# Layer 2 scan: the four blocks of squares of a unit added on GpSimd, one block summed by TensorE instead of four

## What is computed

```python
def mamba2(x, in_w, conv_w, conv_b, dt_bias, A_log, D, gnorm_w, out_w):
    zxbcdt = x @ in_w.T
    z, xBC, dt = ...                       # 512, 512 + 2 * 128 and 8 columns
    dt = softplus(dt + dt_bias)
    xBC = silu(conv(xBC) + conv_b)         # 4 taps along the tokens
    y = ssd(xh, dt, A, B, C) + xh * D[None, None, :, None]
    y = y.reshape(b, l, D_INNER)           # D_INNER = 512
    y = rmsnorm(y * silu(z), gnorm_w)
    return y @ out_w.T

def rmsnorm(x, w):
    return x * rsqrt(mean(x * x, axis=-1) + EPS) * w
```

## Time and profile before

| | |
|---|---|
| time, median of 3 runs | 3643.48 us (3633.23 to 3653.20) |
| span of the profiled execution | 3570.1 us |
| mean granted TensorE clock | 0.932 |
| TensorE, matmul | 3198.0 us busy, 90% |
| TensorE, weight loads | 1856.8 us, 52% |
| VectorE | 2185.0 us, 61% |
| ScalarE | 1801.6 us, 50% |
| GpSimd | 1033.9 us, 29% |
| the scan of layer 2 | about 1735 to 2066 us of the span |

### The profile page before, as it was taken

The page is one execution under the profiler, slowest core; times in us unless marked ns, Lnnn a source line. Parts: engine busy times, 40 slices in busy tenths (PEclk is TensorE's granted clock), DMA queues, the critical chain, the costliest instruction groups (busy, mean ns, idle before and its releaser), DMA issues. The chain is left out here.

```text
span 3570.1 us, 54815 instructions
## 1 busy us (share of the span) xinstructions
PE 3198.0 (90%) x18704; PEld 1856.8 (52%) x18724; DVE 2185.0 (61%) x4458; ACT 1801.6 (50%) x4178; POOL 1033.9 (29%) x1198
## 2 busy tenths in 40 slices
PE   6978849999989899968999988787999999998989
PEld 3655638878756566634456666353233333332656
DVE  4765575455666566675655365335888888884750
ACT  4957723333233344444655444113677777776531
POOL 2535464433350122232444521114111111111300
PEclk8988869999988899998999999898899999999999
DMA  9200056666440000032000041233000000001100
GB/s 333 79 9 1 1 204 199 206 196 187 140 117 1 24 1 1 1 126 85 1 1 1 1 171 48 107 102 106 10 19 19 17 11 19 19 10 50 48 4 21
DMA packets 161108, 240.54 MB, mean 67 GB/s; under 512 B 22771, under 2 KB 136052, under 8 KB 156948
## 3 DMA queue, kind: packets, MB, share of 16 engines
q1 hardware_dynamic: 147012, 199.27, 17.0%
q0 software_dynamic: 13824, 37.77, 3.3%
HBM read 131.97 MB, written 104.99 MB: 66 GB/s over the span
## 5 line engine op out<-in xcount | busy, mean ns | idle before, releaser
L4437 DVE TENSOR_REDUCE peaks<-ps 128x1 f32<-128x1024 f32 x512 | 608.6, 1220 | 152.0 <-PE ps L4379 146.8
L4465 ACT ACTIVATE attn<-ps 128x512 f32<-128x512 f32 x1024 | 535.5, 602 | 118.3 <-PE ps L4370 116.5
L4379 PE MATMUL ps<-keys,queries 96*128 96x512 bf16 x1024 | 391.0, 387 | 5.1 <-DVE peaks L4437 4.9
L4370 PE MATMUL ps<-queries,keys 99*128 99x512 bf16 x1024 | 390.3, 384 | 3.5 <-ACT attn L4465 2.7
L4392 PE MATMUL ps<-attn,head_values 128*32 128x512 f32 x2048 | 272.3, 604 | 0.0
L4370 PEld LDWEIGHTS ps<-queries,keys 99*128 99x128 bf16 x1024 | 99.1, 98 | 306.7 <-ACT attn L4465 222.3
L1187 POOL TENSOR_TENSOR attn_w<-attn_w,attn_share 128x512 f32<-128x512 f32 x128 | 131.7, 1050 | 378.7 <-DVE attn_share L1033 378.7
L2039 PE MATMUL ps<-experts,tileT 128*128 x884 | 228.2, 380 | 0.0
L2240 DVE COPY normed<-ps 128x256 f32<-128x256 f32 x221 | 93.7, 424 | 181.6 <-PE ps L2055 179.7
L4520 POOL CAST peak_parts<-peak 128x4 bf16<-128x4 f32 x64 | 12.3, 193 | 516.6 <-DVE peak L4443 516.6
L2039 PEld LDWEIGHTS ps<-experts,tileT 128*128 128x128 f32 x884 | 151.0, 191 | 15.4 <-issue 0.4
(11 more groups left out here) (697 smaller groups left out, 7106.6 us busy)
## 6 DMA issues: line engine op xcount, KB each, us to landing
tile_in<-routed_rows SPq DMA_DIRECT2D x244, 128.0 KB, 2.3
expert_rows<-normed SPq DMA_DIRECT2D x221, 128.0 KB, 2.2
routed_rows<-zeros SPq DMA_DIRECT2D x2, 8064.0 KB, 45.3
experts<-in_L_ffn_experts SPq DMA_DIRECT2D x4, 3072.0 KB, 20.8
routed_rows<-zeros SPq DMA_DIRECT2D x1, 12160.0 KB, 61.1
kT<-L_xattn_keys SPq DMA_DIRECT2D x8, 1024.0 KB, 7.0
v<-L_xattn_values SPq DMA_DIRECT2D x8, 1024.0 KB, 7.7
experts<-in_L_ffn_experts SPq DMA_DIRECT2D x8, 1024.0 KB
```

The lines of the kernel that those rows point to most:

```text
L4370: nc.tensor.matmul(bank(("score", n)), keys[h % 3][0:DEEP, sl(kt)], queries[h % 3][0:DEEP, sl(c, CHUNK)], start=True, stop=True).then_inc( ...
L4379: last = nc.tensor.matmul(k.ps[:, SB + p % PB, :], queries[h % 3][0:ROWS, sl(t)], keys[h % 3][0:ROWS, sl(c, CHUNK)], start=True, stop=True)
L4437: v.tensor_reduce(peaks[:, r % 2, i // 2, i % 2:i % 2 + 1], k.ps[:, at:at + 2, :], AX.XY, ALU.max).then_inc(s["maxed"], 1)
L4465: nc.scalar.activation(attn[:, n % RING, :], bank(("score", n)), ACT.Exp, scale=1.0 / 16.0).then_inc(s["read"], 1)
```

## The change

`squares` has two blocks instead of four. GpSimd squares block 0 into the first and each further block into the second, which it then adds to the first, so that a unit has seven instructions where it had four (`SQUARINGS = 2 * M - 1`), each with a count on `squared`. Before it squares block 2 or 3 into the second block it waits until the add before has read it; before an add it waits for its square. TensorE waits for all seven and does four products, one for each tile, with the summed block.

```diff
--- before.py
+++ after.py
@@ -3658,7 +3658,8 @@
         inputs = sb(k, stack, "inputs", [P, GROUP, INNER])
         lasting = sb(k, stack, "lasting", [P, HEADS, GROUP, P])
         y = [sb(k, stack, "y", [P, M, GT]) for _ in range(2)]
-        squares = sb(k, stack, "squares", [P, M, GT])
+        squares = sb(k, stack, "squares", [P, 2, GT])
+        SQUARINGS = 2 * M - 1
         scale = [sb(k, stack, "scale", [P, GROUP]) for _ in range(2)]
 
         def is_unit(u):
@@ -3790,12 +3791,11 @@
                     last.then_inc(s["mixed"], 1)
 
                 def square_sums(u):
-                    need(pe, "squared", M * (u + 1))
+                    need(pe, "squared", SQUARINGS * (u + 1))
                     need(pe, "meant", u - 1)
                     for j in range(GROUP):
-                        for m in range(M):
-                            last = nc.tensor.matmul(k.ps[:, 7, 128 + GROUP * (u % 2) + j:129 + GROUP * (u % 2) + j], squares[:, m, sl(j)],
-                                                    k.ones[:, 0:1], start=m == 0, stop=m == M - 1)
+                        last = nc.tensor.matmul(k.ps[:, 7, 128 + GROUP * (u % 2) + j:129 + GROUP * (u % 2) + j], squares[:, 0, sl(j)],
+                                                k.ones[:, 0:1], start=True, stop=True)
                     last.then_inc(s["square_sums"], 1)
 
                 def leave(u, j):
@@ -3938,7 +3938,12 @@
                             if m == 0:
                                 need(pool, "square_sums", u)
                             pool.wait_ge(s["multiplied"], M * u + m + 1)
-                            g_.tensor_tensor(squares[:, m, :], y[u % 2][:, m, :], y[u % 2][:, m, :], ALU.mult).then_inc(s["squared"], 1)
+                            if m >= 2:
+                                pool.wait_ge(s["squared"], SQUARINGS * u + 2 * m - 1)
+                            g_.tensor_tensor(squares[:, min(m, 1), :], y[u % 2][:, m, :], y[u % 2][:, m, :], ALU.mult).then_inc(s["squared"], 1)
+                            if m >= 1:
+                                pool.wait_ge(s["squared"], SQUARINGS * u + 2 * m)
+                                g_.tensor_tensor(squares[:, 0, :], squares[:, 0, :], squares[:, 1, :], ALU.add).then_inc(s["squared"], 1)
 
             @block.vector
             def _(dve):
```

## The result

The changed kernel took 3602.25 us in the median of four runs (3595.79 to 3605.78), the kernel before 3643.69 us beside it; ratio 0.9887, interval 0.9866 to 0.9908. Repeated against the kernel before, it came out at 0.9903 (0.9882 to 0.9924) and 0.9916 (0.9897 to 0.9936). So it is faster by 30 to 41 us. The trace puts 35.2 us of this into the scan.

What follows compares the result with a forecast made beforehand. It took TensorE to bound the layer 2 scan, busy 296.4 of 306 us. Records 14.6, unit 7 and tail 5.0 and clock 11.7 sum to 31.3 us off 3643.5: 3612 us, range 3601 to 3634.

Steps and rivals of the forecast that it cites:

- Removed records: TensorE's sums in the first six units: 8 of 32 records remain, 17.0 us off, 2.4 us back waiting for exponentials.
- The adds: GpSimd, layer 2 scan: 24 adds of 1.27 us, 4.05 us per unit with waits, hidden except behind the last unit.
- Unit 7 and the tail: Last unit and what follows: sums start 1.2 us sooner on GpSimd's chain and shrink by 3.8 us, gaining 5.0 us.
- The clock: Behind the first six sums: TensorE's low clock stretches, 29.2 us with 40% lost, no longer come, gaining 11.7 us.
- The frame: Outside the profiled span: 73.4 us between span and median run time, taken as program start and end, untouched.
- A: TensorE's clock behind the sums falls all the same, not from the sums alone: gain 19.6 us, 3624 us; chance 0.24.
- B: Another chain, VectorE's taps and reciprocal, holds ScalarE's gates in the units: gain 13.4 us, 3630 us; chance 0.13.
- C: GpSimd's adds hold VectorE up in the scan: 11 us longer, 3654 us; chance 0.05.

Runs made afterwards that it cites:

- the wide kernel: The changed kernel with 12 further products of 120 columns, results unused, in each unit's sums: ratio 0.9968 to the kernel before, scan 285.8 us.
- The last version above: Second version for speed: changed kernel, ScalarE takes head 5's exponentials before the next unit's start, VectorE does unit 7's squares and adds: 0.9919, 3539.81 us.
- the pair of narrow and wide products: The changed kernel with 12 further unused products in each unit's sums, of one column (1.0025, scan 302.0 us) or 120 columns (0.9968, scan 285.8 us).
- the first version: The changed kernel with sums behind spread 6 and, in the last unit, TensorE summing each squared block without GpSimd's adds: 0.9920, scan 261.2 us.

## Why the prediction was right

The forecast was 3612 us, 31.3 us less, range 3601 to 3634; the result 3602.25 us is in the range, near its lower end. Of the 10 us between them the scan accounts for 4 us (35.2 against 31.3 us); the other 6 us are within the interval of the first comparison. By its steps:

- **Removed records, 17.0 us less 2.4 us of waiting.** Right, so near 14.6 us. 8 records took 0.88 us, and spread 7 stood idle for 0.71 us where 0.25 us is usual at such a place, so 0.46 us came back and not 0.4: 14.2 us net. That counts 1.0 us by which the clock lengthened two of the old stretches; without it the wide kernel gives 6 x 2.2 = 13.3 us.
- **The adds.** 1270 ns each as taken, and hidden in six units, shown by the kernels with none and with twice as many.
- **Unit 7 and the tail, 5.0 us.** 21.14 - 19.83 + 14.59 - 11.21 = 4.7 us. Near, with both parts a little off. GpSimd's chain as worked out: never idle from the weighting on, and its last add at the end of it. GpSimd's rows of the changed kernel and TensorE's sums behind them:

```profile
2063.78 9.85 POOL L3922 TENSOR_TENSOR lasting<-lasting,pairs 128x512 f32<-128x512 f32 x8 [3.15 <-ACT lasting L3868]
2073.58 1.29 POOL L3937 TENSOR_TENSOR y<-y,gate 128x512 f32<-128x512 f32 x1
...
2085.86 1.26 POOL L3946 TENSOR_TENSOR squares<-squares 128x512 f32<-128x512 f32 x1
```

```profile
2087.17 1.87 PE L3797 MATMUL ps<-ones,squares 128*128 128x1 f32 x8 [4.32 <-POOL squares L3946]
```

The sums themselves took 1.87 us and not 1.3, since the clock is at 0.50 there.

- **The clock, 11.7 us.** The mechanism was right, the size too small. The first six units gained 30.6 us, of which 14.2 us are the records, so the clock gave 16.4 us. Two terms were short. First the price: an odd unit gained 3.86 us, 1.65 us of it for a low stretch of 3.4 us, so 48% and not the 40% that one input product showed (against the wide kernel it is 1.6 us). I had priced only the product; a mix loses more (1.98 against 1.09 us, 45%), which explains a part of it. Second, the falls at the two borders between groups (0.50 from 1841.9), which I had left where they were, were gone too; a fall of 3.4 us there costs 1.6 us. That these went was not forecast and is luck. And the fall was expected to stay away with 8 records: so it does behind the first six sums of every kernel with 8, but not behind the seventh of the changed kernel, which the sum had at nothing. In that unit no input products stand between the spreads. The last version above has the same spreads and the same waits there and no fall, so what decides is open.
- **The frame.** 73.4 us outside the span was wrong, it is 2.0 us; the rest was another chip. It did no harm, as the gain was taken off the median of the runs. The first comparison shows 41 us where the scan gains 35; the other two show 35 and 30, and the interval of the first, 33 to 49 us, holds 35.
- **The rivals.** A was refuted by the pair of narrow and wide products, B and C by the runs with no and with double adds. The chances of the rivals add up to 0.70 for faster and 0.25 for the same, where the prediction has 0.71 and 0.24.

What stays open is the falls at the borders. The changed kernel had none in three profiles on chips of both kinds, nor had the first version; the one without adds, the one with double adds and the second version had one or two, and all kernels with 16 or 32 records had both. For the changed kernel, with three profiles, that is more than chance; of the other kernels there is one profile each, and which moment decides was not isolated.

## What to carry to other kernels

A product with one moving column costs TensorE its weight load, here 0.11 us a record, and then costs again by the clock: 24 such records less per unit saved some 2.2 us directly and 2.4 us by the falls behind them. If an idle engine can fold the operands before TensorE reduces them, that is worth it even where its own add is slow, as long as something still idles behind it at each border. And moving work across a wait helps only if less work then stands ahead of it, so look first at what ends the wait.

## What was not expected of the hardware

120 moving columns in place of one made a float32 record no longer (32 records in 3.56 us either way) and kept the clock at 1.00. And the time of the kernel before differs by 70 to 78 us between chips (3638 to 3644 against 3565 to 3567 us), of which 54 us arise in the stage with the indirect gathers and scatters of layer 0 and 17 us in the attention part of layer 1, so a span of one profile can't be set against times from another chip.
